# Packing two halves of a spline buffer and narrowing the last tile's stationary operand in a graph-network kernel

## What is computed

```
HW  = h @ W;  s = HW @ a[:512];  t = HW @ a[512:]
e   = leaky_relu(s[row] + t[col])
att = softmax of e over the edges of each row
agg = segment_sum(att * h[col], row)
basis = b_splines(agg, grid)              # 8 cubic B-splines per feature
out = silu(agg) @ base_w.T + einsum('nip,oip->no', basis, spline_w)
x   = layernorm(x + out)
```

## Time and profile before

| | us |
|---|---|
| median of 3 runs | 396.26 |
| the 3 runs | 394.77, 396.33, 396.26 |
| profiled execution | 394.77 |
| its span, first to last instruction | 393.0 |
| TensorE busy | 379.8 |
| VectorE busy | 346.1 |
| ScalarE busy | 261.4 |
| GpSimd busy | 35.3 |

### The profile page before, as it was taken

How to read it: one execution, slowest core, us unless ns; L and a number is a source line. 1 busy time by engine, 2 the same in 40 slices (tenths; PEclk the granted TensorE clock), 3 DMA queues, 4 the chain that set the end, 5 groups by cost and what they waited for, 6 DMA issues and landing times.

```text
span 393.0 us, 5049 instructions
## 1 busy us (share of the span) xinstructions
PE 379.8 (97%) x1888; PEld 299.6 (76%) x1888; DVE 346.1 (88%) x438; ACT 261.4 (67%) x251; POOL 35.3 (9%) x88
## 2 busy tenths in 40 slices
PE   5999979999999999999999999999999999999994
PEld 2556647888888888778888888888888888888883
DVE  8999989986787698999899999889999899989445
ACT  1569964755566879865786766777758686866222
POOL 5000310000000001001010101001010101001000
PEclk9999999999999999999999999999999999999999
DMA  7900891000000036549545464623423453633202
GB/s 251 391 16 2 141 274 62 3 0 0 2 0 2 0 108 224 151 127 322 167 123 182 124 166 156 203 66 89 127 60 100 130 170 128 224 92 87 75 27 101
DMA packets 23482, 45.90 MB, mean 117 GB/s; under 512 B 1862, under 2 KB 2074, under 8 KB 23458
## 3 DMA queue, kind: packets, MB, share of 16 engines
q0 software_dynamic: 12400, 24.00, 23.2%
q1 hardware_dynamic: 11058, 21.58, 16.4%
HBM read 43.02 MB, written 2.56 MB: 116 GB/s over the span
## 4 chain that ended last, share of the span: by engine, by line
PE 90%; ACT 5%; DMA 2%; DVE 1%; issue 1%; SPq 0%; DVEq 0%
PE PS L1237 63%; PE PS L1177 17%; PE PS L1115 3%; PE PS L1158 3%; DMA av<-in_a 2%; ACT C L857 2%; PE PS L1045 1%; PE PS L1187 1%; ACT xl L884 1%; ACT Z L862 1%; PE PS L1063 1%; PE PS L1101 1%; PE PS L1095 0%; ACT strow L850 0%; ACT ex L902 0%
## 5 line engine op out<-in xcount | busy, mean ns | idle before, releaser
L1237 PE MATMUL PS<-wh,s 128*128 128x512 f32 x720 | 222.8, 390 | 0.4 <-issue 0.4
L1237 PEld LDWEIGHTS PS<-wh,s 128*128 128x128 f32 x720 | 135.1, 188 | 29.7 <-issue 1.8
L1237 PE MATMUL PS<-wl,s 128*128 128x512 f32 x360 | 140.1, 389 | 0.0
L1237 PEld LDWEIGHTS PS<-wl,s 128*128 128x128 f32 x360 | 67.6, 188 | 13.9
L966 ACT ACTIVATE s<-v 128x1280 fp32r<-128x1280 f32 (+1 forms) x32 | 40.0, 1251 | 40.6 <-DVE v L775 23.8
L949 ACT ACTIVATE v<-xt,bias 128x1280 f32<-128x1280 f32 (+1 forms) x32 | 42.9, 1340 | 20.1 <-DVE s L785 18.7
L769 DVE SCALAR_TENSOR_TENSOR v<-v,v 128x1280 f32<-128x1280 f32 (+1 forms) x32 | 46.4, 1450 | 6.3 <-ACT v L952 6.3
L775 DVE SCALAR_TENSOR_TENSOR v<-v,v 128x1280 f32<-128x1280 f32 (+1 forms) x32 | 46.8, 1461 | 3.7 <-DVE v L771 0.5
L785 DVE SCALAR_TENSOR_TENSOR s<-v,s 128x1280 fp32r<-128x1280 f32 (+1 forms) x32 | 46.5, 1454 | 2.4 <-ACT s L966 2.4
L425 POOL DMA_DIRECT2D wh<-in_splT x32 | 22.9, 715 | 272.2 <-PE PS L1237 172.5
L771 DVE SCALAR_TENSOR_TENSOR v<-v,v 128x1280 f32<-128x1280 f32 (+1 forms) x32 | 46.5, 1453 | 0.0
(11 more groups left out here) (141 smaller groups left out, 347.8 us busy)
## 6 DMA issues: line engine op xcount, KB each, us to landing
wh<-in_splT POOLq DMA_DIRECT2D x32, 512.0 KB, 4.2
wring<-in_splT SPq DMA_DIRECT2D x21, 512.0 KB, 4.0
xt<-in_xT SPq DMA_DIRECT2D x1, 2500.0 KB, 12.3
xh<-in_x POOLq DMA_DIRECT2D x1, 2304.0 KB, 11.6
out<-xr SPq DMA_DIRECT2D x9, 256.0 KB
wh<-in_baseT POOLq DMA_DIRECT2D x4, 512.0 KB, 5.2
xl<-in_x POOLq DMA_DIRECT2D x1, 1536.0 KB, 11.9
wring<-in_baseT SPq DMA_DIRECT2D x3, 512.0 KB, 4.6
```

The costliest lines, as they stand in the source:

```text
L1237: m = e.matmul(PS[:, w % 8, :], sx[:, ic, tl * 128:tl * 128 + 128], wx[:, ic, :], start=first and n == 0, stop=last and n == 2)
```

## The change

Both blocks of a unit's buffers are now packed: in group 1 the second block starts at column 610 (byte 2440 of the buffer), not at column 640 (byte 2560), and an instruction over both blocks covers 1220 adjoining columns. In group 0 the view is the same as before. The separate view with all 640 columns is gone, and the matmuls of tile 9 take 98 columns of the stationary operand and write 98 partitions of PSUM.

```
         def bufs(u):
-            return [t[:, :].rearrange("p (a r) -> p a r", a=2)[:, :, 0:GR[units[u][0]]] for t in vset[u % 3]]
+            return [t[:, 0:2 * GR[units[u][0]]].rearrange("p (a r) -> p a r", a=2) for t in vset[u % 3]]

         def parts(b, u):
-            return whole_parts(b, u)[:, :, 0:GR[units[u][0]]]
-
-        def whole_parts(b, u):
-
-            return b[(u + 2) % NSR][:, :].rearrange("p (a r) -> p a r", a=2)
+            return b[(u + 2) % NSR][:, 0:2 * GR[units[u][0]]].rearrange("p (a r) -> p a r", a=2)
...
-                hi, lo = whole_parts(sh, u), whole_parts(sl, u)
+                hi, lo = parts(sh, u), parts(sl, u)
                 for n, (sx, wx) in enumerate(((hi, wide), (hi, low(u)), (lo, wide))):
-                    m = e.matmul(PS[:, w % 8, :], sx[:, ic, tl * 128:tl * 128 + 128], wx[:, ic, :],
+                    m = e.matmul(PS[0:rows(w), w % 8, :], sx[:, ic, tl * 128:tl * 128 + rows(w)], wx[:, ic, :],
                                  start=first and n == 0, stop=last and n == 2)
```

## The result

The changed kernel takes 398.56 us (median of 6 runs, 397.32 to 398.86), the kernel before 396.14 us (6 runs, 394.77 to 396.33): 1.0060 times as long, 95% interval 1.0041 to 1.0081. It is slower by some 2.4 us, and the time lies outside the range that was given, 394.4 to 397.5 us.

What follows compares the result with a forecast made beforehand. TensorE's unbroken 990 matmuls were taken to bound the kernel; all terms were 0, so 394.77 + 0 + 0 + 0 = 394.77 us, plus 1.49 us for the median gave 396.3 us, range 394.4 to 397.5 us.

Steps and rivals of the forecast that it cites:

- What bounds the kernel: Third stage: TensorE's unbroken 990 matmuls, 225.24 us, set the time; only edits that move their pace count.
- VectorE and ScalarE on packed buffers: Group 1's elementwise instructions over 1220 adjoining elements: at most 62 ns each either way, covered by spare time, 0 on path.
- The second block's address: Group 1's 270 loads from 120 bytes earlier: at worst 212 ns per-column part, under the 226.6 ns pace, so 0.
- Narrowing, the load: Tile 9's 108 loads in group 1: 163 ns instead of 188, 2.7 us less busy, beside matmuls, 0 on path.
- Narrowing, the matmul: Tile 9's 108 matmuls in group 1 still stream 512 columns: taken as 0, with +0.8 and −1.4 us as bounds.
- The nearest rival: Group 1: each of 32 returns from 98 to 128 columns costs 24 ns, +0.8 us, 397.1 us; chance 0.27.
- The rival that the 13.3 ns shrink with the width: Tile 9's matmuls: their unexplained time beyond 213.3 ns streaming shrinks, 0.3 to 1.4 us faster, down to 394.9; chance 0.06.
- The rivals that the load becomes the bound: Group 1's loads stop hiding: 65 width changes at 100 ns, +6.5 us, 402.8 us, chance 0.06; a second form, chance 0.02.
- The fast-load rival: Tile 9's 98-column loads lose a fast form and take 325 ns: +10.6 us, 406.9 us; chance 0.02.
- The sum: Whole kernel: 394.77 + 0 + 0 + 0 = 394.77 us, the median forecast at 396.3 us.
- +0.8 end: Upper bound for tile 9's matmuls: 32 returns to 128 columns at 24 ns each, 0.8 us.
- The forecast's own sign: Test in the third stage: the prediction is wrong if the stretch of 990 matmuls differs by more than 1 us.

Runs made afterwards that it cites:

- write610: Kernel before, but ScalarE and VectorE write packed (second block at column 610) while TensorE's loads read from column 640: 6800 ns a unit of group 1, as before.
- pack610: Kernel before with only the packing (group 1's second block at column 610, tile 9 kept at 128 columns): 398.46 us, 1.0068 times the kernel before.
- read610: Kernel before, but TensorE's loads of block 1 in group 1 read from column 610, writes unchanged: 6918.7 ns a unit against 6800.
- narrow98: Kernel before with only the narrowing (tile 9 with 98 columns, second block kept at column 640): 398.09 us, 1.0050 times the kernel before.
- narrow100: Kernel before with tile 9 at 100 columns, second block kept at column 640: 395.17 us, 0.9998 times the kernel before.
- rows128: Kernel before, but the tenth step of the attention sums contracts over 128 rows instead of 98, added rows zeroed: 1.0005 times the kernel before.
- all98: Kernel before with all five tiles of group 1 at 98 columns, nodes left out: 6867 ns a unit against 6800.
- all64: Kernel before with all five tiles of group 1 at 64 columns, nodes left out: 6900 ns a unit against 6800.
- fixed: The change with both sizes rounded up (second block at column 612, tile 9 with 100 columns): 397.12 us, 1.0034 times the kernel before.

## Why the prediction was wrong, point by point

**What bounds the kernel:** right. TensorE's stretch is the path; +2.66 us in it made a span 2.7 us longer.

**VectorE and ScalarE on packed buffers, 0:** right; 1422 and 1301 ns, and in write610 the packed writes alone leave the stretch at 225.21 us.

**The second block's address, "even this end stays hidden":** this is the step that failed most. Its bounds were put on the duration of the load, and a load shorter than 226.6 ns was taken to cost nothing. pack610 and read610 show 2.28 us from that address alone with loads of 188 ns. The bound was on the wrong quantity: what moved was the distance between matmuls, which the forecast took as given though it had left 13.3 ns of it unexplained.

**Narrowing, the load, 0 on the path:** the size was right (163 ns forecast, 162 to 167 measured, 2.6 us less busy), and the same error stands behind the 0.

**Narrowing, the matmul, 0:** wrong; narrow98 shows +1.95 us. The nearest rival (each return to 128 columns costs) had the place of the loss right, with 24 ns for a return from the earlier trace rows; narrow98 has 60 ns. It is not a rule for every width: narrow100 makes the same returns for nothing. The forecast set aside for the earlier trace rows. But the earlier trace rows show what it costs to enter a series of matmuls, to 10 ns; the loss is in the eight matmuls after it, a few ns each, and only a row that spans them, like the earlier trace rows, can show it. rows128 shows that the 98 rows caused those 24 ns.

**The rival that the 13.3 ns shrink with the width:** it did not happen. With all five tiles narrowed the matmuls are 228.9 ns apart at 98 columns and 230 at 64 (all98, all64), no nearer to each other than before.

**The rivals that the load becomes the bound:** they did not happen and were rightly given little. No distance in group 1 of the changed kernel passed 239 ns, where 100 ns a change were priced. The fast-load rival with its four times longer load did not happen either: a 98-column load is 25 ns shorter. The Trainium skill ("TensorE: Matmul & The Clock Gate", section on weight-path perf modes) excepts FP32 from the fast weight load and does not say whether the rounded type counts as FP32; the trace, where no load grew, is as if it did.

**The sum:** the two terms that were set to 0 are 2.28 and 1.95 us, and overlap to 2.66 us. The forecast's own +0.8 end held only the second, at less than half its size, so the range ended at 397.5 us, 1.1 us short. By the forecast's own sign, a stretch of 990 that differs by more than 1 us, it was wrong as well.

Not settled is why one start column or width is free and its neighbour not. Neither multiples of 16, 32, 64 or 128 bytes, nor where the load ends, nor the number of columns sorts the table, and fixed shows that start and width count together. Two things were not separated. The weights were never moved (in every kernel the buffers of weights and of values lie multiples of 1024 bytes apart), so whether the start column counts by itself or against the place of the weights is open. And a narrower load came always with fewer partitions written in PSUM, so the loss of narrow98 may belong to either; for the start column read610 leaves only the load. What is shown is where the loss sits (the distance between matmuls while such loads run beside them, and up to eight or so after) and what does not cause it (the other engines, longer loads, the clock).

## What to carry to other kernels

Where back-to-back matmuls set the time, the start column and the width of the stationary operand are part of their pace, even when every load is shorter than a matmul: here 15 matmuls took between 3398 and 3501 ns by that alone. Leave a layout whose distances are even in the trace as it is, or measure each size that replaces it; rounding both up to four elements was not enough. And when a bound says "hidden", ask of which quantity: a transfer can be hidden in duration and still change the rhythm of what hides it.

## What the runs showed of the hardware that was not expected

- Rounded-f32 matmuls of 512 columns ran 226.7 ns apart in their steadiest stretches, bf16 ones of 500 columns 212 ns: 15 matmuls in 3.34 us, (3.34 − 0.37) / 14 = 212 ns, in the kernel before:

```profile
51.55 3.34 PE L1101 MATMUL PS<-nought 128*128 128x500 bf16 x15 [2.40 <-DVE tmax L673]
```

  The Trainium skill ("TensorE: Matmul & The Clock Gate", section "Back-to-back issue gap") gives 512 / 2.4 + 2.5, about 216 ns, for an isolated matmul of 512 columns, and about 131 ns for each in a stream of loads and matmuls. The bf16 rows, each matmul with its load, agree with the first form (an estimate by it for 500 columns is 211 ns); the rounded-f32 ones of this case are 11 ns above it. No row here comes near 131 ns, and the measurement decides.
- Narrower loads did not speed the stream: on average 226.7 ns at 128 columns, 228.9 at 98, 230 at 64, with loads of 188, 163 and 134 ns.
- After a disturbance the distances follow nearly the same series (233 to 236, 224, 231, 236, 228, 233, 231, then 227), seen after a stall, after transposes and after a narrow tile. The whole series loses some 38 ns, but the stream can enter it later or not at all: in the kernel before, the distances after the first one of unit 3 (307 ns) are 229, 233, 236, 224, 231, 236, 228, 233, 231, after that of unit 0 (314 ns) 233, 231, 226, and after that of unit 6 (310 ns) 227 at once; block 0 of pack610 enters at 236, 228, 233, 231. So what a disturbance costs varies by where it leaves the stream in this series.
- Disturbances from two causes did not add: start column 610 and 98 columns cost 119 and 118 ns a unit alone and 144 together; start column 612 and 100 columns cost 0 and 0 alone and 51 together.
